# Row maxima in a tile of their own, a norm's scale applied behind its projection, and new instruction orders in a four-layer decoder kernel

## The reference, cut to what matters

```python
x = x + xattn(layernorm(x), ctx, seg, ...)     # x: (2, 256, 256) f32
x = x + window_attn(layernorm(x), ...)
x = x + quantised_ffn(layernorm(x), ...)

# xattn: 4 layers, H = 16 heads of 16, D = 256, F = 1024
h = rmsnorm(x, n1[l])                          # x * rsqrt(mean(x*x) + eps) * w
q, k, v = split(h @ Wqkv[l].T + bqkv[l]); q, k = rope(q), rope(k)
x = x + softmax(q k.T * scale + causal) v @ Wo[l].T + bo[l]
h2 = rmsnorm(x, n2[l])
x = x + softmax(h2 Wq_c.T kc.T * scale + cross_mask) vc @ Wo_c[l].T   # 4096 context rows
h3 = rmsnorm(x, n3[l])
x = x + silu(h3 @ Wg[l].T) * (h3 @ Wu[l].T) @ Wd[l].T
```

## Time and profile before

| | |
|---|---|
| median of 3 runs | 620.34 us (619.81 to 621.71) |
| span of the profiled execution, first to last instruction | 617.9 us |
| what lies between that span and the median | 2.4 us |
| mean granted TensorE clock | 0.991 |

### The profile page before, as it was taken

One profiled execution on the slowest core, in us unless ns is written; L12 is line 12 of the kernel. 1 busy time (PEld: TensorE's weight loads), 2 busy tenths in 40 slices (PEclk: granted clock), 3 DMA queues, 4 the chain that ended last, 5 costly groups with the idle time before them and its releaser, 6 DMA issues.

```text
span 617.9 us, 13676 instructions
## 1 busy us (share of the span) xinstructions
PE 564.1 (91%) x5806; PEld 421.8 (68%) x5806; DVE 353.5 (57%) x680; ACT 279.5 (45%) x490; POOL 117.7 (19%) x124
## 2 busy tenths in 40 slices
PE   4989998999999899999998989999898989999855
PEld 1666655988767566988766658987666558897523
DVE  5896445466564454674554455574554364752787
ACT  0254444633355336433544446342554547445523
POOL 4252100012323100020612000122312001252110
PEclk9999999999999999999999999999999999999969
DMA  8800020010500200201400200204000200000001
GB/s 334 345 2 25 12 69 2 5 65 1 205 2 4 102 1 3 68 1 27 180 1 36 70 2 2 69 1 189 16 2 1 71 0 2 0 1 2 2 1 39
DMA packets 4676, 30.29 MB, mean 49 GB/s; under 512 B 1153, under 2 KB 1665, under 8 KB 2818
## 3 DMA queue, kind: packets, MB, share of 16 engines
q1 hardware_dynamic: 4610, 29.35, 12.5%
HBM read 28.82 MB, written 0.52 MB: 47 GB/s over the span
## 4 chain that ended last, share of the span: by engine, by line
PE 77%; DVE 10%; ACT 8%; issue 3%; POOL 1%; DMA 1%; SPq 0%; DVEq 0%; POOLq 0%
PE psD L326 18%; PE QD L621 12%; PE psD L634 9%; PE QD L408 6%; PE QD L443 4%; ACT PTR L1253 3%; PE psD L320 3%; PE QD L436 3%; PE QD L394 3%; DVE AQ L1803 3%; PE psD L463 2%; PE QD L431 2%; PE psD L359 2%; PE psD L484 2%; PE psD L470 2%
## 5 line engine op out<-in xcount | busy, mean ns | idle before, releaser
L1253 ACT ACTIVATE PTR<-QD 128x2048 f32<-128x2048 f32 x40 | 75.1, 1878 | 41.8 <-PE QD L443 21.5
L326 PE MATMUL psD<-WAB,hT 128*128 128x256 f32 (+1 forms) x216 | 70.1, 465 | 2.2 <-DVE hT L1744 2.2
L2492 POOL TENSOR_TENSOR rstd<-ms,mhalf 128x2 f32<-128x2 f32 x26 | 19.9, 764 | 271.8 <-DVE ms L1729 270.6
L1803 DVE TENSOR_REDUCE AQ<-QD 128x8 f32<-128x2048 f32 (+1 forms) x24 | 55.0, 2290 | 27.0 <-PE QD L408 27.0
L621 PE MATMUL QD<-HH,WFH 128*128 128x256 f32 x224 | 67.4, 301 | 0.4 <-DVE WFL L1903 0.4
L1903 DVE TENSOR_TENSOR WFL<-WC,WFH 128x512 fp32r<-128x512 f32 x64 | 48.0, 755 | 32.2 <-ACT WFH L1297 32.1
L621 PE MATMUL QD<-HL,WFH 128*128 128x256 f32 x224 | 63.3, 283 | 0.0
L621 PE MATMUL QD<-HH,WFL 128*128 128x256 f32 x224 | 63.3, 283 | 0.0
L1800 DVE TENSOR_REDUCE AQ<-QD 128x16 f32<-128x2048 f32 x16 | 36.7, 2293 | 39.9 <-PE QD L408 39.9
L634 PE MATMUL psD<-WC,HID 128*128 128x256 f32 x256 | 58.2, 380 | 0.0
L326 PEld LDWEIGHTS psD<-WAB,hT 128*128 128x128 f32 x216 | 39.7, 195 | 21.0 <-issue 14.2
(11 more groups left out here) (172 smaller groups left out, 1021.2 us busy)
## 6 DMA issues: line engine op xcount, KB each, us to landing
WC<-in_wc SPq DMA_DIRECT2D x4, 3072.0 KB, 10.9
WAB<-in_wa SPq DMA_DIRECT2D x4, 1024.0 KB, 4.9
WAB<-in_wb SPq DMA_DIRECT2D x4, 1024.0 KB, 4.7
WF<-in_wf SPq DMA_DIRECT2D x1, 3072.0 KB, 22.8
bias<-in_bias SPq DMA_DIRECT2D x4, 512.0 KB, 3.4
WAB<-in_wt SPq DMA_DIRECT2D x1, 1024.0 KB, 6.0
X<-in_x SPq DMA_DIRECT2D x2, 256.0 KB, 2.8
out_x<-X SPq DMA_DIRECT2D x4, 128.0 KB, 2.4
```

Source lines behind the costliest of these rows:

```text
L326: mm = pe.matmul(bank(l, use)[:, col:col + n], lhs(k), rhs(k), start=(k == 0), stop=(k == KT - 1))
L1253: nc.scalar.activation(PTR[:, r % 2, :], QD[:, :], ACT.Exp, scale=SCALE).then_inc(t_exp, 1)
L1803: v = dve.tensor_reduce(QKR[b][:, t, 0, h, MAXROW].rearrange("p (s r) -> p r s", r=SG_H), QD[:, :].rearrange("p (r s n) -> p r s n", r=4, ...
```

## The change

- **Maxima.** `maxima` writes into a new zeroed tile MX: for each of the four strips of a partition group there is a row of its own, MAXROW + s, so that one 128x128 transpose for a query tile holds the maxima of eight or sixteen heads. `maxima_T` makes 1 transpose a round in self attention and 2 in cross attention. The keys have their 1 in row MAXROW + s for strip s.
- **Query strips with maxima.** `query_max_strips` goes from ACT to DVE: it adds the transposed maxima (PSUM, broadcast over the strips) to the query strips that stand in QKT (SBUF), into Q2. The memsets that cleared MAXROW in the queries go.
- **Norms 0 and 1.** `normalise` is left only for norm 2. `norm_T` transposes X itself as soon as the residual is in; the scale of a token is multiplied in by `biased_qk`, `biased_v` and `cross_q`, which wait for rstd.
- **Start.** DVE subtracts the mean (`centre`), PE transposes that; `first_scale` joins the two norms' scales; `layernorm_apply` to X comes later, behind `masks`. `pads` has one larger memset and four short ones for each batch more.
- **Orders.** The lists of all engines are new. `masks` moves behind `maxima(0, 4)`; `mask_by_key` on PE stands ahead of `scores(0, 5)`; the first three `sum_abs` of layer 3 are no longer in a row ahead of `self_strips`; in the tail `window_middle_v(1)` (DVE) moves ahead of `window_gamma(0)`.

```diff
@@ PE: norm_T, maxima_T
-                pe.wait_ge(h_set[b], l * NORMS + i + 1)
-                transposes(l, f"n{i}{b}", hs[:, 2 * b:2 * b + 2, :])
+                if i == 2:
+                    pe.wait_ge(h_set[b], l + 1)
+                elif i == 1:
+                    pe.wait_ge(*emptied(l, f"wo{b}"))
+                elif l == 0:
+                    pe.wait_ge(x_set[b], 1)
+                else:
+                    pe.wait_ge(*emptied(l - 1, f"y{b}"))
+                transposes(l, f"n{i}{b}", (hs if i == 2 or l == i == 0 else X)[:, 2 * b:2 * b + 2, :])
...
-                blocks = [(q, s) for s in ss for q in (range(QT) if cross else (t,))]
-                for n, (q, s) in enumerate(blocks):
-                    mm = pe.transpose(bank(l, use)[:, n * P:(n + 1) * P], block_of(b, q, 0, s), ident)
+                for n, q in enumerate(range(QT) if cross else (t,)):
+                    mm = pe.transpose(bank(l, use)[:, n * P:(n + 1) * P], MX[:, b, q, ss[0] // 2, :], ident)
@@ ACT
-            def query_max_strips(l, r):
...
-                nc.scalar.activation(Q2[:, 0:n], bank(l, use)[:, 0:n], ACT.Copy).then_inc(free(l, use), 1)
@@ DVE
+                dve.wait_ge(rstd_set[b], l * NORMS + 1)
                 dve.wait_ge(*filled(l, use))
-                dve.tensor_tensor(QK[b][:, t, :], bank(l, use)[:, :], bias[:, 0:2 * D], ALU.add).then_inc(free(l, use), 1)
+                dve.scalar_tensor_tensor(QK[b][:, t, :], bank(l, use)[:, :], (rstd if l else rs0)[:, b, t:t + 1], bias[:, 0:2 * D], ALU.mult, ALU.add)\
+                   .then_inc(free(l, use), 1)
...
+            def query_max_strips(l, r):
+
+                use = f"q2_{r}"
+                cross, b, t, ss = round_of(r)
+                n = L if cross else P
+                at = 0 if cross else t * P
+                dve.wait_ge(*filled(l, use))
+                dve.tensor_tensor(Q2[:, 0:len(ss) * n].rearrange("p (s n) -> p s n", n=n), QKT[b][:, ss[0]:ss[-1] + 1, at:at + n],
+                                  bank(l, use)[:, 0:n].unsqueeze(1).broadcast_to([P, len(ss), n]), ALU.add).then_inc(free(l, use), 1)
...
-                no_maxima(b)
-                dve.tensor_copy(QKR[b][:, :, 0, :, 0:HD], bank(l, use)[:, :].rearrange("p (t h d) -> p t h d", t=QT, h=H))\
-                   .then_inc(free(l, use), 1)
+                dve.wait_ge(rstd_set[b], l * NORMS + 2)
+                for t in range(QT):
+                    v = dve.tensor_scalar(QKR[b][:, t, 0, :, 0:HD], bank(l, use)[:, t * D:(t + 1) * D].rearrange("p (h d) -> p h d", h=H),
+                                          rstd[:, B + b, t:t + 1], None, ALU.mult)
+                v.then_inc(free(l, use), 1)
...
+            def centre(b):
+                for t in range(QT):
+                    v = dve.tensor_scalar(hs[:, 2 * b + t, :], X0[:, 2 * b + t, :], mv[:, b, t, 0:1], None, ALU.subtract)
+                v.then_inc(x_set[b], 1)
@@ POOL: pads
-                    pool.memset(rest[:, :, MAXROW + 1:STRIP], 0.0)
-                    pool.memset(QKR[b][:, :, 1, :, MAXROW], 1.0)
+                    pool.memset(rest[:, :, MAXROW:STRIP], 0.0)
+                    pool.memset(MX[:, b, :, :, :], 0.0).then_inc(pads_step, 1)
+                    pool.wait_ge(pads_step, b + 1)
+                    for s in range(4):
+                        pool.memset(QKR[b][:, :, 1, SG_H * s:SG_H * (s + 1), MAXROW + s], 1.0)
@@ ACT, layer(): the middle of self attention
-                squares(l, 1, 0)
-                query_max_strips(l, 4)
                 strip_outputs(l, 3)
-                split_high(l, 1)
                 key_strips(l, 0)
-                query_max_strips(l, 5)
+                squares(l, 1, 0)
                 exp(l, 4)
                 exp(l, 5)
                 query_strips(l, 0, 0)
+                query_strips(l, 0, 1)
@@ DVE, layer()
                 maxima(l, 7)
+                query_max_strips(l, 6)
+                query_max_strips(l, 7)
                 residual(l, 1, "wo1")
@@ DVE, layer 0, and the list of the last layer
                 maxima(0, 4)
+            masks()
+            cross_kv(0, 0)
+            layernorm_apply(1, 1, X0, X, lambda v: v.then_inc(x_kept[1], 1))
+            query_max_strips(0, 4)
+            layernorm_apply(0, 0, X0, X, lambda v: v.then_inc(x_kept[0], 1))
+            mask_by_key()
+            maxima(0, 5)
...
                 maxima(NL - 1, 0)
                 maxima(NL - 1, 1)
+                query_max_strips(NL - 1, 0)
```

More of the change, by code:

```diff
@@ L834, in layer @@
                 out_proj(l, 1, "cwo1", Woc, "coT1")
+                down(l, 0, range(0, 4))
                 gate_up(l, 0, 7)
-                down(l, 0, range(0, 4))
                 norm_T(l, 2, 1)
@@ L1102, in rest @@
                 out_proj(NL - 1, 1, "cwo1", Woc, "coT1")
+                down(NL - 1, 0, range(0, 4))
                 gate_up(NL - 1, 0, 7)
-                down(NL - 1, 0, range(0, 4))
                 norm_T(NL - 1, 2, 1)
@@ L1112, in rest @@
                 gate_up(NL - 1, 1, 5)
+                down(NL - 1, 1, range(0, 4))
                 gate_up(NL - 1, 1, 6)
                 gate_up(NL - 1, 1, 7)
-                down(NL - 1, 1, range(0, 4))
                 window_T(0)
@@ L1485, in _ @@
             strip_outputs(0, 2)
+            self_strips(0, 1, 1, 1)
+            exp(0, 3)
             copy_oT(0, 0, "oT0")
-            query_max_strips(0, 3)
-            self_strips(0, 1, 1, 1)
-            split_high(0, 0)
-            exp(0, 3)
-            query_max_strips(0, 4)
             squares(0, 1, 0)
+            exp(0, 4)
             strip_outputs(0, 3)
-            exp(0, 4)
-            query_max_strips(0, 5)
             key_strips(0, 0)
@@ L2105, in layer @@
                 divide(l, 2)
+                query_max_strips(l, 3)
                 maxima(l, 4)
+                query_max_strips(l, 4)
+                cross_kv(l, 0)
                 residual(l, 0, "wo0")
-                cross_kv(l, 0)
+                maxima(l, 5)
+                weigh_T(l, 1, 0)
                 mean_square(l, 1, 0)
-                maxima(l, 5)
-                normalise(l, 1, 0)
-                weigh_T(l, 1, 0)
+                query_max_strips(l, 5)
+                cross_q(l, 0)
                 divide(l, 3)
-                cross_q(l, 0)
+                split_low(l, 0)
                 maxima(l, 6)
@@ L2341, in rest @@
                 divide(NL - 1, 2)
+                query_max_strips(NL - 1, 3)
                 maxima(NL - 1, 4)
+                query_max_strips(NL - 1, 4)
+                cross_kv(NL - 1, 0)
                 residual(NL - 1, 0, "wo0")
-                cross_kv(NL - 1, 0)
+                maxima(NL - 1, 5)
                 mean_square(NL - 1, 1, 0)
-                maxima(NL - 1, 5)
-                normalise(NL - 1, 1, 0)
                 weigh_T(NL - 1, 1, 0)
+                query_max_strips(NL - 1, 5)
+                cross_q(NL - 1, 0)
                 divide(NL - 1, 3)
-                cross_q(NL - 1, 0)
                 maxima(NL - 1, 6)
@@ L2370, in rest @@
                 mean_square(NL - 1, 2, 0)
-                normalise(NL - 1, 2, 0)
+                normalise(NL - 1, 0)
+                query_max_strips(NL - 1, 9)
+                weigh_T(NL - 1, 2, 0)
                 split_low(NL - 1, 2)
-                weigh_T(NL - 1, 2, 0)
                 tokens_high(NL - 1, 0)
@@ L2432, in rest @@
                 layernorm_stats(4, 0, X)
+                window_middle_v(1)
                 window_gamma(0)
```

645 lines of the change are left out of this document (318 added, 327 removed).

## The result

The changed kernel takes 615.19 us (median of 4 runs, 614.64 to 616.54) beside 620.94 us of the kernel before on the same chip: ratio 0.9903, 95% interval 0.9879 to 0.9927. That is faster by 1.0%; the forecast was 2.0%. The profiled execution spans 613.4 us, 4.5 less than 617.9, where the sum had 12.6 less: 8.1 us are missing.

The account below looks back on a forecast made before the run. PE was taken as the bound, with QD second in attention and a DVE chain in the tail. Start -0.4, layer 0 -1.98 and -0.5, layers 1 and 2 -6.2, layer 3 -4.5, tail +1.0: -12.6, so 607.7 us, range 601 to 617.5.

Parts of the forecast that it names:

- Transposes, 1.98 us a layer: In each layer, 18 fewer transposes of the maxima at 0.11 us each on PE save 1.98 us.
- QD is the bound: Rival: in attention PE's saved 7.9 us turn into waits for reductions and exps; 615.6 us (613 to 618.5), chance 0.17.
- Exp order, 1.1 us a layer: In attention, no query copy stands ahead of an exp in ACT's list, so exp(4) comes sooner: 1.1 us a layer.
- the sum 3.1: The forecast gain of each of layers 1 and 2: -3.1 us.
- The add costs nothing beside it: DVE's query add replacing ACT's copy was put at 0 (up to 2.8 us in all), included in the exp-order gain.
- this rival: Query adds wait behind a 2.29 us reduction: 628 with nine late rounds, chance 0.08; three to six cancel, 618.5 to 622.2, 0.08.
- Start -0.4: At the start, a shorter path to PE's first instruction less the larger pads: net -0.4 us, from -1.5 to 0.
- Layer 0, -2.9 in all: Start and layer 0 up to residual y0: -0.4 for the start, -1.98 for transposes, -0.5 for exp order.
- The masks, put at 0: In layer 0, moving masks costs some 2.5 us of PE idle and wins as much: 0, from -2.5 to +2.5.
- Layer 3, -4.5: In layer 3, -3.1 us as in layers 1 and 2, and -1.4 for spreading three sum_abs ahead of self_strips.
- Tail +1.0: In the tail, window_middle_v(1) ahead of window_gamma(0) on DVE waits for a late projection: +1.0 us (0 to 1.5).
- Flow: The forecast case: PE's saved work and ACT's order both show in the time; 607.7 us (602 to 613), chance 0.55.

Follow-up runs that it names:

- e5: The changed kernel with the saved transposes put back as idle ones, 18 more a layer: 619.18 us, ratio 0.9967.
- e6: The changed kernel's functions in the old instruction lists, query additions on VectorE, three of them placed behind the next round's reduction: 622.14 us, ratio 1.0015.
- e7: The changed kernel with exp_table ahead of the first self_strips in ScalarE's list, as in the kernel before: 614.74 us, ratio 0.9883.
- e14: e9 with value_pads behind scale_ternary(0), scale_ternary(1) behind add_beta(1), and values(0, 1) on TensorE ahead of scores_T(0, 1): 607.52 us, ratio 0.9790.
- e11: e9 with masks and mask_by_key back in their places of the kernel before: 611.16 us, ratio 0.9855.
- e12: e9 with the first three sum_abs of layer 3 again in a row ahead of self_strips: 609.97 us, ratio 0.9841.
- e10: e9 with window_middle_v(1) back behind layernorm_stats(6, 0), and POOL's add_bo(0, 0) moved behind causal(0, 3): 609.98 us, ratio 0.9831.
- e1: The changed kernel with POOL's tail reordered: value_pads behind norm 2's last rsqrt, both scale_ternary behind add_beta(0): 611.52 us, ratio 0.9841.
- e2: The changed kernel with value_pads alone moved behind the last rsqrt of norm 2: 612.12 us, ratio 0.9867.
- e3: The kernel before with value_pads and scale_ternary(1) moved right behind ln_rsqrt(2), as the changed kernel has them: 623.52 us, ratio 1.0040.
- e9: The changed kernel with e1's POOL order, e7's early table load, and VectorE's wait for pads moved behind weigh_T(0, 0, 0): 610.27 us, ratio 0.9821.

## Why the prediction was wrong

It had the sign and, for the steady layers, the size; 615.19 lies in its range at the upper end. The predicted change was over twice the measured one. The missing 8.1 us are +3.9 in layer 0, +0.4 in layers 1 and 2, -1.7 in layer 3, +5.0 between y0 and y1, and +0.5 behind. By its steps:

- **Transposes, 1.98 us a layer: about half.** PE's work fell as forecast, but only 0.9 us a layer are time (e5). The step "PE flows in 75.95 of 81.20 us" took a busy engine for a bound one. The rival "QD is the bound" isn't borne out for the other half: what grew is mostly the waits for oT and hs, and in layer 1 those ahead of a write to QD fell from 2.77 to 1.11 us.
- **Exp order, 1.1 us a layer: the gain of the lists is nearer 2.** Layers 1 and 2 give 2.9; without the transposes 2.0 remain. Between exp(1, 3) and exp(1, 4) layer 1 takes 7.43 us instead of 8.61, so 1.2 stand where I said. That the sum 3.1 fits 2.9 comes from two errors that cancel.
- **The add costs nothing beside it: only with new lists.** There no wait of PE for a query add stands in layers 1 to 3; in the old lists such waits are 2.08 us of layer 1, and the gain is gone (e6). The prediction also priced this rival wrongly: by its own 2.29 us a round, three rounds give 614.6 and not 618.5, which takes 4.7.
- **Start -0.4:** PE starts 0.74 us sooner, but the first scores 0.73 later. I had read the new lists for what stands ahead of an exp and not for ScalarE's table load: the step "SP's DMAs are issued as before" looked at the wrong engine. It cost 1.4 us (e7).
- **Layer 0, -2.9 in all: the first failed step, +1.0, off by 3.9.** Shown: table load 1.4, transposes 1.98 - 0.88 = 1.1, the values' place 0.4 (e14). The masks, put at 0, gained 1.4 (e11), so that some 2.4 us are still without a shown cause: PE idles 131.26 - 114.33 = 16.93 us up to y0 before and 132.26 - 111.12 = 21.14 after. Most of it has a place: exp(0, 5) to exp(0, 6) takes 18.61 us, before 16.85 (rows below).
- **Layer 3, -4.5, measured -6.2.** The sums' spreading is right (1.6 against 1.4, e12); 1.7 more come from other parts of its list, not tested. Exp(3, 7) to exp(3, 9) takes 19.51 us instead of 22.01, where layer 1 has 20.93 instead of 21.41.
- **Tail +1.0: the second failed step, +6.55.** The term itself was 0.1 (e10). What I left out is POOL's list: I weighed the shared port for the masks and gave it no price where `value_pads` and `scale_ternary` moved right behind `ln_rsqrt(2)`, that is, beside the very instruction that waits for `ln_rsqrt(2)`. It costs 5.0 us, 3.6 as PE's wait and most of the rest as low clock (e1, e2, e3). Of the 1.5 us from y1 to the end, DVE's steps show 0.2 up to 58 us behind y1; the rest falls in the last products, at a granted clock of 0.88 from 50 to 58 us behind y1, before 1.00. No run shows its cause, and e9, e11 and e12, with the same lists there, need 65.5, 66.6 and 64.7 us for this stage.

The place in layer 0, PE before, then after:

```profile
77.47 1.99 PE L326 MATMUL psD<-WAB,oT 128*128 128x256 f32 x8 [0.25 <-ACT oT L1265]
79.30 1.03 PE L431 MATMUL QD<-maskT,identB 128*128 128x512 bf16 x4
...
78.42 1.99 PE L329 MATMUL psD<-WAB,oT 128*128 128x256 f32 x8
80.25 0.60 PE L532 MATMUL psD<-const,AQ 128*128 128x128 f32 x4
81.50 0.66 PE L323 MATMUL psD<-const,X 128*128 128x128 f32 x4 [0.65 <-DVE X L1819]
81.99 1.03 PE L440 MATMUL QD<-maskT,identB 128*128 128x512 bf16 x4
```

Where the old list has the scores by key of round 6 (QD) right behind the output projection (psD<-WAB,oT), the new one has the transposes of `cross_kT` and `norm_T(0, 1, 1)` between, and the latter wait for a residual. From projection to scores by key that is 3.57 instead of 1.83 us. No run moved these entries.

The likeliest case in the prediction was Flow. Neither it nor the QD rival is what happened: half of the transposes' time in the layers, and outside of them two mechanisms that no case had, the table load and the port. That the time lands at QD's 615.6 is chance. The forecast of 607.7 is nearly met by e14, 607.52, which mends those two and the values' place, but by other terms.

## What to carry to other kernels

When lists are rewritten, read every moved instruction of every engine, POOL's memsets and scales and ScalarE's table loads too, and ask what runs beside it and what waits for that. A saved piece of a busy engine is not yet time: here it was worth half, and only a run with the piece put back as idle work could say so. And look at a wait on TensorE's path for what comes after it: here 3.63 us of wait cost 1.7 more in clock, and most of a gain made at the start vanished in it.

## What the runs showed of the hardware

- Two POOL memsets of 128x1536, 1.38 us each, which read nothing, hold a pair of VectorE tensor_scalar from SBUF to SBUF: 2.85 instead of 0.61 us (e1). With a POOL tensor_scalar of 2.00 us behind them the pair takes 4.73 us: its first instruction (2.75 us) ends 0.14 us behind the second memset, so it didn't get in between the memsets, and its second (2.05) ends 0.13 behind the tensor_scalar.
- A POOL select of 128x2048 (2.21 us) holds such a pair too: 2.08 instead of 0.73 us (e10).
- The same wait of 3.63 us was followed by a low clock of different length: the sixteen products behind it took 5.30 us in one trace and 6.06 in another whose start alone was changed. Behind waits of 1.28 (e2) and 2.71 us (e3) in that place they took 3.62.
- The clock behind the first wait for scores, 1.76 us long, differs between executions of the same code: 0.66 or 1.00 from 20 to 25 us, worth 1.6 us.
